# Visits' one-hots made one visit at a time, between the sums into the accumulators, in a graph layer with experts

## What is computed

```python
def _L0_gnn_ref(x, edge_index, edge_attr, ...):
    src = edge_index[0]
    ...
    edge_proj = edge_attr @ W_sum + b_sum
    sum3d = jax.ops.segment_sum(edge_proj, src, num_segments=num_nodes)
    ...
    return x + z_in[in_deg] + z_out[out_deg] + cent_term + vor_term + sum3d
...
    xn = _layernorm(x, axis=-1)
    x = x + _L0_gnn_ref(xn, ...) + _L0_mix_ref(xn[None], ...)[0]
    x = x + _L0_ffn_ref(_layernorm(x, axis=-1)[None], ...)[0]
```

## Time and profile before

| | us |
|---|---|
| median of 3 runs | 2529.84 (2528.25 to 2530.05) |
| the profiled execution | 2511.43 |
| its span | 2509.7 |
| TensorE busy with matmuls | 1656.7 (66%) |
| VectorE busy | 1395.1 (56%) |
| ScalarE busy | 739.9 (29%) |
| GpSimd busy | 1349.8 (54%) |
| the sums, line 1188 | 169.5, 592 instructions |
| the one-hots by VectorE, line 1201 | 151.8, 124 instructions |
| the visits' matmuls, line 699 | 299.0 |

### The profile page before, as it was taken

How to read it: one execution, slowest core, us unless ns; L and a number is a source line. 1 busy time by engine, 2 the same in 40 slices (tenths; PEclk the granted TensorE clock), 3 DMA queues, 4 the chain that set the end, 5 groups by cost and what they waited for, 6 DMA issues and landing times.

```text
span 2509.7 us, 37689 instructions
## 1 busy us (share of the span) xinstructions
PE 1656.7 (66%) x11883; PEld 1320.7 (53%) x11883; DVE 1395.1 (56%) x3342; ACT 739.9 (29%) x1615; POOL 1349.8 (54%) x1290
## 2 busy tenths in 40 slices
PE   4313424554455334515699998777957999999997
PEld 0001313332223212303588887677845898888886
DVE  5345213432345323413688876877995666666664
ACT  0000112221222111301054443067743443344342
POOL 5474757767677667667200018820004676667664
PEclk9955657776677667757799999999967999999999
DMA  8232434444445444433244559987154998999995
GB/s 267 74 89 67 118 106 128 145 127 132 141 133 151 126 134 124 118 110 89 67 123 133 131 144 240 265 229 199 66 185 140 275 269 266 275 263 268 269 266 150
DMA packets 380659, 414.34 MB, mean 165 GB/s; under 512 B 50006, under 2 KB 295438, under 8 KB 380462
## 3 DMA queue, kind: packets, MB, share of 16 engines
q1 hardware_dynamic: 220120, 218.17, 28.8%
q0 software_dynamic: 57952, 92.15, 14.6%
q10 hardware_dynamic: 102390, 101.63, 13.9%
HBM read 316.11 MB, written 95.67 MB: 164 GB/s over the span
## 4 chain that ended last, share of the span: by engine, by line
PE 30%; DVE 13%; issue 7%; another core or an unknown queue 2%; ACTq 2%; ACT 1%; DVEq 1%; DMA 1%; SPq 0%; POOL 0%; POOLq 0%
PE bank L926 11%; PE bank L940 11%; DVE big L1188 3%; PE bank L699 3%; DVE big L1201 2%; DVE hotB L1233 1%; ACTq L2053 1%; PE bank L912 1%; DVE hotA L1231 1%; PE bank L679 1%; DVEq L1188 1%; PE bank L840 1%; DVE stats L1452 1%; DVE big L1209 1%
## 5 line engine op out<-in xcount | busy, mean ns | idle before, releaser
L1893 POOL DMA_INDIRECT sorted_rows<-edge_rows,sorted_pos x780 | 800.4, 1026 | 387.0 <-issue 221.8
L806 PE MATMUL bank<-mixw,xnT 128*128 128x512 f32 x392 | 234.7, 754 | 303.1 <-ACT mixw L1747 160.8
L1845 ACT ACTIVATE mixw<-bank,edge_rows 128x256 f32<-128x256 f32 (+1 forms) x456 | 238.5, 549 | 341.6 <-PE bank L926 191.4
L806 PEld LDWEIGHTS bank<-mixw,xnT 128*128 128x128 f32 x392 | 92.3, 248 | 417.1 <-issue 416.6
L926 PE MATMUL bank<-edge_rows,big 128*128 128x256 f16 (+1 forms) x2736 | 293.0, 266 | 11.1 <-issue 8.6
L940 PE MATMUL bank<-big 128*128 128x256 f16 x2520 | 284.4, 273 | 1.0 <-issue 1.0
L926 PEld LDWEIGHTS bank<-edge_rows,big 128*128 128x128 f16 x2736 | 250.1, 98 | 45.7 <-issue 10.4
L1956 POOL DMA_INDIRECT state<-xn_rows,edge_rows x105 | 116.5, 1110 | 274.8 <-DVE edge_rows L1584 243.1
L940 PEld LDWEIGHTS bank<-big 128*128 128x128 f16 x2520 | 244.2, 98 | 28.5 <-issue 1.3
L1978 POOL DMA_INDIRECT result<-mixw,edge_rows x105 | 173.2, 1650 | 139.5 <-DVE mixw L1626 76.2
L1188 DVE TENSOR_TENSOR big<-big,bank 128x128 f32 x592 | 169.5, 286 | 94.7 <-remote 14.0
(11 more groups left out here) (362 smaller groups left out, 2860.5 us busy)
## 6 DMA issues: line engine op xcount, KB each, us to landing
big<-w_parts SPq DMA_DIRECT2D x114, 1024.0 KB
edge_rows<-edge_attr SPq DMA_DIRECT2D x78, 640.0 KB
big<-sorted_rows ACTq DMA_DIRECT2D x296, 129.0 KB
big<-sorted_rows SPq DMA_DIRECT2D x128, 129.0 KB
big<-L_ffn_W ACTq DMA_DIRECT2D x128, 128.0 KB
w_parts<-big ACTq DMA_DIRECT2D x64, 256.0 KB
mixw<-sorted_rows ACTq DMA_DIRECT2D x104, 129.0 KB
sorted_rows<-edge_rows,sorted_pos POOLq DMA_INDIRECT x780
```

The costliest lines, as they stand in the source:

```text
L806: ins = e.matmul(ps_kv[h], xnT[:, t % 2, k, :], kvw[:, k, h * INNER:(h + 1) * INNER], start=(k == 0), stop=(k == KC - 1))
L1845: e.activation(h32[:, h, w], ps_h[h % 4][:, w], ACT.Gelu, bias=m_r[:, n, h:h + 1], scale=m_r[:, n, HC:HC + 1]).then_inc(gelu_done, 1)
L1893: e.indirect_dma_start(sorted_rows, bass.IndirectOffsetOnAxis(ap=row_pos[:, c:c + 1], axis=0), rows, None, bounds_check=last_row, oob_is_e ...
```

## The change

VectorE makes a batch's one-hots by four instructions of 128x256, one for each visit, in place of one of 128x1024. Each adds one to `visit_hot_made`, which now counts visits. The four sums of batch `v - 4` are put between them: in the early order the first sum, the key, then one-hot 0, sum 1, one-hot 1, sum 2, one-hot 2, sum 3, one-hot 3; in the late order the key, then one-hot 0, sum 0 and so on to one-hot 3, sum 3. The load of the registers moves to the head of the step. TensorE waits ahead of each visit's two matmuls for that visit's one-hots. Batches whose one-hots ScalarE makes are left as they were, and in the steps where VectorE makes none the four sums follow each other as before.

```diff
@@ tensor_visit
-        else:
-            e.wait_ge(visit_hot_made, b + 1 - scalar_hots(b))
...
         for i in range(VB):
+            if not by_scalar(b):
+                e.wait_ge(visit_hot_made, VB * (b - scalar_hots(b)) + i + 1)
             for k in range(VROWS):
                 ins = e.matmul(ps_visit[b % 2][:, i * P:(i + 1) * P], visit_rows[visit_slot(b)[0]][:, i, k, 0:EDIM],
                                hot_of(b)[:, i, k, :], start=(k == 0), stop=(k == VROWS - 1))
@@ vector_visit
-        if v - 2 >= SYNC_FROM + 2:
-            vector_visit_hots(e, v, lanes)
-            vector_visit_sums(e, v - 4, regs)
-        else:
-            vector_visit_sums(e, v - 4, regs)
-            vector_visit_hots(e, v, lanes)
+        b = v - 4
+        sums = range(VB * b, VB * (b + 1)) if 0 <= b < BATCHES else ()
+        if sums:
+            e.load(regs, visit_i[OFF_ROW:OFF_ROW + 1, VB * b:VB * (b + 1)])
+        late = v - 2 >= SYNC_FROM + 2
+        if sums and not late:
+            vector_visit_sum(e, sums[0], regs)
+        hots = vector_visit_keys(e, v)
+        for i in range(VB):
+            if hots:
+                vector_visit_hot(e, v - 2, i, lanes)
+            j = i if late else i + 1
+            if j < len(sums):
+                vector_visit_sum(e, sums[j], regs)
+
+    def vector_visit_sum(e, n, regs):
+        b, i = divmod(n, VB)
+        if i == 0:
+            e.wait_ge(visit_summed, b + 1)
+        o = e.snap(regs[i], min_val=0, max_val=TILES * P)
+        if n == 0:
+            e.wait_ge(visit_scalar, 1)
+        else:
+            e.wait_ge(acc_added, n)
+        e.tensor_tensor(acc[:, bass.ds(o, P)], acc[:, bass.ds(o, P)], ps_visit[b % 2][:, i * P:(i + 1) * P],
+                        ALU.add).then_inc(acc_added, 1)
+
+    def vector_visit_keys(e, v):
+        if by_scalar(v - 1):
+            vector_key(e, v - 1)
+        b = v - 2
+        if not 0 <= b < BATCHES or by_scalar(b):
+            return False
+        vector_key(e, b)
+        if b >= 2:
+            e.wait_ge(visit_summed, hot_free(b))
+        e.wait_ge(visit_keyed, b + 1 + by_scalar(b + 1))
+        return True
+
+    def vector_visit_hot(e, b, i, lanes):
+        e.tensor_tensor(hot_of(b)[:, i], lanes.unsqueeze(1).to_broadcast([P, VROWS, P]),
+                        visit_key[:, b % 4, i].unsqueeze(2).to_broadcast([P, VROWS, P]), ALU.is_equal).then_inc(visit_hot_made, 1)
```

## The result

The changed kernel takes 2498.61 us (median of 4 runs, 2497.0 to 2504.08), the kernel before beside it 2529.05 (4 runs, 2515.83 to 2530.05): a ratio of 0.9907, with a 95% interval of 0.9881 to 0.9932. Forecast were 2504 us and a range of 2492 to 2523.

The account below looks back on a forecast made before the run. VectorE was taken as the bound, with TensorE from 1256 to 1490 us, except 1490 to 1557 (ScalarE's queue the largest part). -11 - 1 - 9 - 5 = -26 us from the 2529.8 us median gives 2504; range 2492 to 2523.

Parts of the forecast that it names:

- A sum costs 0.20 us more when it waits for the one ahead: VectorE's visit steps: three waits of 0.20 us between sums, hidden by one-hots between them, 0.60 us less per batch.
- Four one-hots cost 0.18 more than one: VectorE's one-hots: four take 1.32 us instead of 1.14, 0.18 more; net -0.42 us per batch.
- The register load is hidden in the early order and bare in the late one: Load at the step's head: nothing lost in the early order; late, a loss counted, from 0.2 to about 0.5 us.
- TensorE's wait for each visit is worth nothing: TensorE's waits ahead of each visit's matmuls: next to nothing gained, nothing counted for gain or cost.
- 1256 to 1557: Two stretches: to 1490 us TensorE becomes the bound, -11 (0 to -14); then VectorE not the bound, -1 (0 to -3).
- 1557 to 1642: Stretch bound by VectorE alone: 12 us less on VectorE, some lost near the transfer-rate edge: -9, bounds -2 and -12.
- 1642 to 1761: Late stretch of 24 pairs, VectorE the bound: 4.44 to 4.63 us a pair against 4.80; -5, bounds 0 and -9.
- Before 1256 us: Visits before the first stretch: VectorE is busy 61 of 121 us and waits for others, so gain 0.
- Of the rivals, the first: Stretches from 1256 us on: TensorE and the transfers take the gain; -8 us, 2522 us; chance 0.10.
- The second: VectorE's steps: the register load is bare in every step; -9 us, 2521 us; chance 0.08.
- The third: VectorE's sums: the 0.41 us between them is the engine's own, not the wait's; +18 us, 2548 us; chance 0.06.
- the fourth: Whole kernel: no change that can be measured, within 5 us of 2530; chance 0.06.

Follow-up runs that it names:

- e1: Kernel before with four one-hots and TensorE's wait for each visit, sums kept together in the old order, not interleaved: 1.0054 of the kernel before.
- e5: The changed kernel, unaltered, run again on a machine where the kernel before takes 1908 us: 0.9973 of the kernel before.
- e2: The changed kernel, but TensorE waits once per batch for all four visits' one-hots: 0.9982 of the kernel before.
- e3: The changed kernel, but from batch 100 on each transfer of a visit's rows brings half the bytes, as many transfers: one run, 1905.0 us.
- e4: The changed kernel, but from batch 100 on only rows of visits 0 and 2 are brought, half the transfers and bytes: one run, 1903.1 us.
- e10: The changed kernel, but ScalarE starts one of the eight transfers of a late pair, two steps ahead: 0.9977 of the kernel before.
- e12: As e10, but late steps keep the old order (four one-hots, register load, four sums): 2463.44 us against 2490.12 for the kernel before, ratio 0.985.
- e7: The changed kernel, but ScalarE starts one of the eight transfers of a late pair, one step ahead of its key: 1.0202 of the kernel before.
- e11: The changed kernel with the register load written twice at each step's head; only one load is in the trace: one run, 1906.69 us.

## Why the prediction was right, step by step

- *A sum costs 0.20 us more when it waits for the one ahead.* Right: 3.05 against 2.39 us for the same instructions in two orders (e1, e5, undisturbed steps), 0.66, against 0.60 predicted. Four sums in a row take 1.45 us to the next key, four alone 4 x 0.195 = 0.78; that is the 0.67.
- *Four one-hots cost 0.18 more than one.* Right: 0.19 in e1. The net of an undisturbed step is -0.47 us instead of -0.42; the sum gives way after 0.19 to 0.20 instead of 0.22 when a one-hot follows.
- *The register load is hidden in the early order and bare in the late one.* Right by the rows: 0.26 us to spare there, 0.28 us lost here.
- *TensorE's wait for each visit is worth nothing.* Right: e2 against e5, and e1.
- *1256 to 1557: -12 us, since TensorE takes over as the bound.* Right. The rest stage, whose state additions span 281.0 us before (1273.2 to 1554.2) and 268.3 after (1284.1 to 1552.4), is 12.7 us shorter, with TensorE busy 98% of the first stretch. That is just beyond the 12 forecast for the two stretches, within their bounds.
- *1557 to 1642: -9 us, with some loss to the transfers.* 30 batches at 2.57 instead of 2.96 us: 0.39 x 29 = 11 us. The engines did 296 GB/s at a share of 1.07, and no wait of a key for its rows is in the trace from 1556 to 1630 us. So the loss that I had put down for the transfers did not come; a smaller one came in its place, with the sums' six waits for TensorE (3.1 us) in it.
- *1642 to 1761: -5 us.* This step failed: nothing was gained, 5.05 us a pair against 4.91. "VectorE bounds again" was read from one pair near 1705 us; over the stretch before, SyncE's queue took 4.96 us for the eight transfers of a pair and lived on its lead. The prediction had the queue at 4.33 to 4.9 us a pair and took VectorE's 4.44 to 4.63 as the later. The 4.33 is a slip: it takes the two gaps of rows 10 for short, but they are 1.18 and 0.20 us, and 1715.34 - 1701.38 = 13.96 us for three pairs make 4.65, not 13.0 and 4.33. Both values of the queue, 4.65 and 4.9, were thus later than VectorE's, and the measured one is 5.06. VectorE's own term was right (4.5 to 4.7 us once the queue is relieved, 4.44 to 4.63 predicted), with its parts: fourth sum to key, load between them, 1093.77 - 1093.26 = 0.51 (0.50 predicted), fourth interleaved sum to the next group 1092.03 - 1091.55 = 0.48 (0.41 to 0.60). From the rest stage's end to the last sum the gain was 8.4 us, not 14.
- *Before 1256 us: 0.* From the scatter's end to the first state addition it took 3.7 us less. I have no run that tells this from chance.

-3.7 - 12.7 - 8.4 = -24.8 us, against -26. That the sums come so near is in part luck: 3.7 us come from a stretch for which nothing was forecast, and they make up for the last stretch, where 5 us were forecast and none came. Without them it is 21 us. The inner range of the prediction, 2494 to 2514, is not what its bounds taken by halves give (-38 and -2 around -26: 2498 to 2516). Of the rivals, the first was half true, in a place that it did not name: the transfers took the gain of the last stretch, by their starting and not by their bytes (e3, e4, e10). The second falls with the 0.33 us behind the fourth one-hot: it is true of the late order only. The third falls with e1 against e5, and the fourth with the interval.

## What to carry to other kernels

Short instructions that wait for one another on one engine can each leave it idle for a while (0.20 us a sum here). Independent work between them hides that, if it lasts until the next one is due: here 0.33 us of one-hot did, where 0.21 were open. The test in a trace is the spacing of starts when the follower waits (0.41) and when it does not (0.20). Splitting a long instruction to get such filler has its price, about 0.06 us for each further piece here; count the pairs that are still adjacent, over the step's boundary too. And before a gain is booked, add up the queue that feeds the stage over the whole stretch, not over one pair: starting the transfers, not their bytes, held it at 0.63 us each, and a lead in buffers had hidden it until the engine got faster.

## What the runs showed of the hardware

- The same program took 2529, 1908 (on three machines) and 2490 us. The difference lies in the first 1200 us of the span, before and beside the scatter. In the traces of the 2529 us machine, PE, DVE and ACT stand still together there again and again, up to 56 us at a time before and 35 after, mostly with no releaser on the core (ScalarE waits 141.8 us for "remote" from 600 to 1000 us in the kernel before); on the 1908 us machines ScalarE has no such wait there and PE is busy 934 of the first 1200 us instead of 505. On the 2490 us machine it is busy 513 (e12). From 1250 us on the stages look alike. What holds the engines was not found. The change's worth differs with it: 0.9907 on the 2529 us machine, where the visits end after the gathers of neighbour rows (last sum at 1751.4, last gather started at 1645.6), 0.9973 where they end before them (1164.1 and 1239.5).
- A single transfer's start takes 0.34 us on ScalarE's queue (e7); in a row, with the register work for each address, SyncE starts one in 0.52 us (8 in 4.00 us), and in 0.62 to 0.63 over a long stretch. In e11 a load of registers whose values are overwritten before they are read has no record in the trace: an experiment that doubles a cost has to be checked for the double.
